# A fifth set of single-row transfers, an own buffer for tile 0, and the diagonals made on VectorE

## The reference

```python
x = x + elu(softmax(leaky(e_src + e_dst) masked by adj) @ (layernorm(x) @ W))
h = layernorm(x)                          # 8 batches of 1024 tokens
scores, idx = product_key_top16(h)        # of 128 + 128 keys: 16 of 16384 rows, per token and head
w = softmax(scores)
k = sum(w[j] * keys_table[idx[j]] for j in range(16))      # per token and head, 128 wide
v = sum(w[j] * values_table[idx[j]] for j in range(16))
x = x + causal_attention(h @ Wq, k, v) @ Wo                # 8 heads, 1024 tokens
```

## Time and profile before

| | |
|---|---|
| time, median of 3 runs | 10059.12 us (10057.98 to 10074.63) |
| profiled execution, its span | 10059.9 us |
| GpSimd busy | 7544.0 us, 75% |
| VectorE busy | 6956.2 us, 69% |
| TensorE matmuls busy | 5726.9 us, 57% |
| ScalarE busy, without issuing DMAs | 3087.9 us, 31% |
| DMA engines' mean busy share | 39% in a steady head |

### The profile page before, as it was taken

One profiled execution on the slowest core, in us unless ns is written; L12 is line 12 of the kernel. 1 busy time (PEld: TensorE's weight loads), 2 busy tenths in 40 slices (PEclk: granted clock), 3 DMA queues, 4 the chain that ended last, 5 costly groups with the idle time before them and its releaser, 6 DMA issues.

```text
span 10059.9 us, 190416 instructions
## 1 busy us (share of the span) xinstructions
PE 5726.9 (57%) x23108; PEld 4551.2 (45%) x23108; DVE 6956.2 (69%) x42844; ACT 3087.9 (31%) x9770; POOL 7544.0 (75%) x7957
## 2 busy tenths in 40 slices
PE   5655555555555555555555555555555555555555
PEld 4544444444444444444444444444444444444444
DVE  8876667666666677676776666767667676666664
ACT  4333233233333333333333333333333332322222
POOL 5777777777777777777777777777777777777776
PEclk7877777777777777777777777777777777777777
DMA  3333343333433334333343333333333333333333
GB/s 109 105 109 109 109 114 109 109 109 109 113 109 109 109 109 113 109 109 109 109 113 109 109 109 109 113 109 109 109 111 111 110 109 109 109 111 109 109 109 100
DMA packets 503669, 1100.92 MB, mean 109 GB/s; under 512 B 196992, under 2 KB 246912, under 8 KB 502144
## 3 DMA queue, kind: packets, MB, share of 16 engines
q0 software_dynamic: 381120, 1041.22, 36.4%
q1 hardware_dynamic: 71488, 31.70, 1.3%
q10 hardware_dynamic: 49664, 16.42, 0.8%
HBM read 1084.36 MB, written 4.19 MB: 108 GB/s over the span
## 4 chain that ended last, share of the span: by engine, by line
POOL 73%; issue 24%; DVE 1%; PE 1%; POOLq 0%; DMA 0%; ACT 0%; ACTq 0%; SPq 0%; DVEq 0%
POOL ring L353 73%; DVE hot L1013 0%; DMA wo<-in_Wo 0%; POOLq L369 0%; PE ps_o L724 0%; ACTq L492 0%; POOLq L367 0%; DVE ps_v L935 0%; DMA ring<-in_table,idx 0%; PE ps_p L610 0%; PE ps_p L614 0%; DVE nmax L1064 0%; PE ps_s L748 0%; POOLq L368 0%; DVE cand L987 0%
## 5 line engine op out<-in xcount | busy, mean ns | idle before, releaser
L353 POOL DMA_INDIRECT ring<-in_table,idx x7940 | 7542.5, 950 | 2491.2 <-issue 2420.6
L671 PE MATMUL ps_w<-ring,diag 128*128 128x256 f32 x8192 | 2151.7, 423 | 13.0 <-issue 8.7
L715 PE MATMUL ps_p<-ident,prob 128*128 128x128 f32 x2304 | 564.7, 400 | 2304.0 <-ACT prob L453 2296.3
L671 PEld LDWEIGHTS ps_w<-ring,diag 128*128 128x128 f32 x8192 | 1740.6, 218 | 297.1 <-issue 19.7
L1013 DVE SCALAR_TENSOR_TENSOR hot<-rank,posf,cand 128x54 f32<-128x54 f32 x8192 | 1654.5, 271 | 0.3
L715 PEld LDWEIGHTS ps_p<-ident,prob 128*128 128x128 f32 x2304 | 395.1, 202 | 2501.0 <-ACT prob L453 1600.2
L932 DVE TENSOR_SCALAR ps_v<-ring,wgt 128x256 f32<-128x256 f32 x512 | 248.4, 485 | 1837.0 <-DMA ring<-in_table,idx 1836.8
L935 DVE SCALAR_TENSOR_TENSOR ps_v<-ring,wgt,ps_v 128x256 f32<-128x256 f32 x3072 | 1478.9, 481 | 19.6
L444 ACT ACTIVATE diag<-ident,wgt 128x128 f32<-128x128 f32 x4096 | 1251.8, 391 | 0.0
L453 ACT ACTIVATE prob<-ps_s,nmax 128x128 f32<-128x128 f32 (+7 forms) x512 | 378.1, 738 | 2300.8 <-issue 2259.6
L724 PEld LDWEIGHTS ps_o<-probT,kv 128*128 128x128 f32 x4608 | 986.7, 304 | 144.9 <-ACT probT L461 81.6
(11 more groups left out here) (119 smaller groups left out, 8141.2 us busy)
## 6 DMA issues: line engine op xcount, KB each, us to landing
far<-in_table SPq DMA_DIRECT2D x16352, 1.0 KB
far<-in_table ACTq DMA_DIRECT2D x15904, 1.0 KB
ring<-in_table,idx POOLq DMA_INDIRECT x7940
xin<-in_x SPq DMA_DIRECT2D x8, 512.0 KB
mask<-in_adj SPq DMA_DIRECT2D x1, 4096.0 KB, 15.9
out_x<-acc SPq DMA_DIRECT2D x64, 64.0 KB
far_row<-far_at SPq DMA_DIRECT2D x128, 0.5 KB
far_row<-far_at ACTq DMA_DIRECT2D x124, 0.5 KB
```

The source lines that it names most:

```text
L353: pool.indirect_dma_start(out=ring[:, t % RING, k, :], out_offset=None, in_=table, in_offset=bass.IndirectOffsetOnAxis(ap=idx[:, t, k:k + ...
L671: ins = nc.tensor.matmul(pw_ps, diag[:, k, :], ring[:, t % RING, k, :], start=(k == 0), stop=(k == PE_ROWS - 1))
L715: ins = nc.tensor.transpose(ps_p[:, c, (j % 4) * P:(j % 4 + 1) * P], prob[:, j * P:(j + 1) * P], ident[:])
```

## The change

- SETS are five tiles: 1, 6, 0, 4 and 3. SyncE fetches tile 1 (128 rows), 96 rows of tile 3, and tile 6 (128 rows); it asks for the next set's addresses ahead of the last 32 rows of the one it fetches. ScalarE fetches tiles 0 and 4 and 32 rows of tile 3, 36 rows in each unit, as 20 and 16 with a register load for each; they are issued in portions of 8 between its other work of the unit (some, with TURNING, TURNED and SUMMING), the rest at the unit's end. ScalarE does this in the first head as well, from unit 4 on.
- The sum of tile 0 is written to kv_first, not to kv[:, 0, :]. ScalarE copies its values to kv later in the unit (keep_first), VectorE's wait for the last product moves to t = 1, and TensorE's last product stands behind turn_keys at t = 0 as at the others.
- VectorE makes all eight diagonals of a unit in one product of 128 x 1024, right behind sum_rows; ScalarE makes none.
- stores and load of SyncE stand at other places of the turn from batch to batch.

```diff
-FAR = (3, 7)
-NEAR = (0, 4)
-SETS = FAR + NEAR
-NEAR_UNITS = 4
+SETS = (1, 6, 0, 4, 3)
+SP_ORDER = (0, 4, 1)
+SP_STOP = {0: P, 4: 96, 1: P}
+SP_FIRST_ORDER = (2, 0, 4, 1)
+NEAR_BEGIN = {1: 2, 4: 4, 5: 3}
+NEAR_PARTS = {1: ((2, 0, (20, 16)),), 2: ((2, 36, (20, 16)),), 3: ((2, 72, (20, 16)),),
+              4: ((2, 108, (20,)), (4, 96, (16,))),
+              5: ((3, 0, (20, 16)),), 6: ((3, 36, (20, 16)),), 7: ((3, 72, (20, 16)),),
+              0: ((3, 108, (20,)), (4, 112, (16,)))}
+ACT_BEGINS = tuple(NEAR_BEGIN.values())
+FIRST_SETS = (3, 4)
+FIRST_UNITS = (4, 5, 6, 7)
+TURNING = 8
+TURNED = 8
+SUMMING = 8
...
+        def made(t):
+
+            return kv[:, t, :] if t else kv_first[:]
...
-            def far_fetch(n, i, stop=P):
+            def far_fetch(n, i, following=None):
...
+                stop = SP_STOP.get(i, P)
                 for q in range(0, stop, LOADED):
+                    if q == stop - LOADED and following and following[1] not in ACT_BEGINS:
+                        far_begin(*following)
...
+            def turn(b, more):
+                n = (b + 1) * HEADS
+                far_fetch(n, SP_ORDER[0], (n, SP_ORDER[1]))
+                if more:
+                    load(b + 2)
+                far_fetch(n, SP_ORDER[1], (n, SP_ORDER[2]))
+                far_fetch(n, SP_ORDER[2], (n + 1, SP_ORDER[0]))
                 stores(b)
...
-            def diagonals(n, t):
-
-                act.wait_ge(pw_mm, n * UNITS + t)
-                act.wait_ge(wgt_ready, n * UNITS + t + 1)
-                for k in range(PE_ROWS):
-                    nc.scalar.mul(diag[:, k, :], ident[:], wgt[:, t, k:k + 1]).then_inc(diag_ready, 1)
...
+            def keep_first():
+
+                nc.scalar.copy(kv[:, 0, P:KV], kv_first[:, P:KV]).then_inc(first_kept, 1)
...
+                    for rows in loads:
+                        _, at = nc.values_load_multi_w_load_instructions(
+                            far_row[0:1, i, start:start + rows], engines=[mybir.EngineType.Activation],
...
+                    some(fetch, TURNING)
                     if t or not first:
                         attend_turned(*behind)
+                    some(fetch, TURNED)
                     if ahead:
                         choose_softmax((n + 1) * UNITS + t)
                     attend_begin(n, t)
...
+                    some(fetch, SUMMING)
                     if t or not first:
                         attend_out(*behind)
+                    if t == 0:
+                        keep_first()
...
+                    some(fetch, P)
...
-                pe.wait_ge(diag_ready, (u + 1) * PE_ROWS)
+                pe.wait_ge(diag_ready, u + 1)
...
+                if t == 1:
+                    pe.wait_ge(first_kept, n + 1)
...
-                if t == 0:
+                if t == 1:
 
                     dve.wait_ge(o_mm, n * UNITS)
                 after(row_sum[0])
-                nc.vector.tensor_tensor(kv[:, t, :], part[:], pw_ps, ALU.add).then_inc(rows_summed, 1)
+                nc.vector.tensor_tensor(made(t), part[:], pw_ps, ALU.add).then_inc(rows_summed, 1)
...
+            def diagonals(n, t):
+
+                dve.wait_ge(pw_mm, n * UNITS + t)
+                dve.wait_ge(wgt_ready, n * UNITS + t + 1)
+                nc.vector.tensor_tensor(diag[:], ident[:].unsqueeze(1).broadcast_to([P, PE_ROWS, P]),
+                                        wgt[:, t, 0:PE_ROWS].unsqueeze(2).broadcast_to([P, PE_ROWS, P]),
+                                        ALU.mult).then_inc(diag_ready, 1)
...
                         sum_rows(n, t)
+                        diagonals(n if t < UNITS - 1 else n + 1, (t + 1) % UNITS)
                         choose_rows(t, a_unit, c)
```

More of the change, by code:

```diff
@@ L1 @@
+import itertools
 from contextlib import ExitStack
@@ L295, in far_fetch, with far_sets @@
                             .then_inc(far_dma[i], 16)
[L297 to L308, removed]
+            def far_sets(n, order, follows):
+                for i, after_it in zip(order, order[1:] + (follows,)):
+                    if i == order[-1]:
+                        far_fetch(n, i, None if follows is None else (n + 1, follows))
+                    else:
+                        far_fetch(n, i, (n, after_it))
@@ L315, in _ @@
[L315 to L321, removed]
+            far_begin(1, SP_FIRST_ORDER[0])
+            far_sets(1, SP_FIRST_ORDER, SP_ORDER[0])
             with sp.Fori(2, HEADS) as h:
-                far_sets(h, range(len(FAR)))
+                far_sets(h, SP_ORDER, SP_ORDER[0])
             with sp.Fori(0, BATCH - 2) as b:
-                load(b + 2)
-                turn(b)
+                turn(b, True)
@@ L327, in _ @@
                 with sp.Fori(1, HEADS) as h:
-                    far_sets((b + 1) * HEADS + h, range(len(FAR)))
-            turn(BATCH - 2)
+                    far_sets((b + 1) * HEADS + h, SP_ORDER, SP_ORDER[0])
+            turn(BATCH - 2, False)
             with sp.Fori(1, HEADS - 1) as h:
-                far_sets((BATCH - 1) * HEADS + h, range(len(FAR)))
-            far_sets(BATCH * HEADS - 1, range(len(FAR)), True)
+                far_sets((BATCH - 1) * HEADS + h, SP_ORDER, SP_ORDER[0])
@@ L473, in near_begin, with near_fetch, some @@
                     act.dma_start(far_row[0:1, i, :], far_at[:, i:i + 1]).then_inc(far_row_dma[i], 16)
-            def near_load(n, i, part):
-                if part in (0, NEAR_UNITS - 1):
+            def near_fetch(n, t, first):
+                for i, start, loads in NEAR_PARTS[t]:
+                    if first and (t not in FIRST_UNITS or i not in FIRST_SETS):
+                        continue
                     act.wait_ge(far_row_dma[i], n * 16)
                     act.sem_inc(act_mark, 1)
[L480 to L493, removed]
+                    if not (isinstance(n, int) and n == 1):
+                        act.wait_ge(rows_summed, (n - 1) * UNITS + SETS[i] + 1)
+                        act.sem_inc(act_mark, 1)
+                    for rows in loads:
+                        _, at = nc.values_load_multi_w_load_instructions(
+                            far_row[0:1, i, start:start + rows], engines=[mybir.EngineType.Activation],
+                            min_val=0, max_val=(HEADS * NUM_KV - 1) * KV_BYTES,
+                            skip_runtime_bounds_check_because="made of two positions below 128 and a head below 8")
+                        for j in range(rows):
+                            yield act.dma_start(far[start + j:start + j + 1, i, :].bitcast(U8),
+                                                table_bytes[bass.ds(at[j], KV_BYTES)]).then_inc(far_dma[i], 16)
+                        start += rows
+            def some(fetch, rows):
+                for _ in itertools.islice(fetch, rows):
+                    pass
             act.wait_ge(aux_mm, 1)
@@ L537, in head @@
                         graph_keep(b + 1, h, g)
-                    if ahead and t in (1, 1 + NEAR_UNITS) and not first:
-                        near_begin(n + 1, len(FAR) + t // NEAR_UNITS)
+                    if ahead and t in NEAR_BEGIN and not (first and NEAR_BEGIN[t] not in FIRST_SETS):
+                        near_begin(n + 1, NEAR_BEGIN[t])
+                    fetch = iter(())
+                    if ahead or t == 0:
+                        fetch = near_fetch(n + 1 if t else n, t, first)
                     if ahead:
@@ L548, in head @@
                     attend_begin(n, t)
[L549 to L555, removed]
-                        near = len(FAR) + (t - 1) % UNITS // NEAR_UNITS
-                        part = (t - 1) % NEAR_UNITS
-                        at = near_load(n + 1 if t else n, near, part)
-                        near_rows(near, part, at, range(0, HIDDEN))
+                    some(fetch, SUMMING)
                     if t or not first:
                         attend_out(*behind)
+                    if t == 0:
+                        keep_first()
                     if ahead:
@@ L567, in head @@
                         graph_copy(g)
-                    if fetch:
-                        near_rows(near, part, at, range(HIDDEN, LOADED))
+                    some(fetch, P)
                 if not ahead:
@@ L682, in turn_keys @@
                     pe.wait_ge(g_xnT_copied, graph_rows[0])
-                nc.tensor.transpose(ps_t[:, 0, :], kv[:, t, 0:P], ident[:]).then_inc(k_tp, 1)
+                nc.tensor.transpose(ps_t[:, 0, :], made(t)[:, 0:P], ident[:]).then_inc(k_tp, 1)
             def scores(n, t):
@@ L722, in attend_sum @@
                 pe.wait_ge(p_copied, halves(n, t) + HALVES[t])
+                if t == 1:
+                    pe.wait_ge(first_kept, n + 1)
                 for j in range(t + 1):
-                    ins = nc.tensor.matmul(oT_ps, kv[:, j, P:KV], probT[:, j * P:(j + 1) * P],
+                    values = kv[:, j, P:KV] if t else kv_first[:, P:KV]
```

(9 more changed lines are left out.)

10 lines of the change are left out of this document (3 added, 7 removed).

## The result

The changed kernel takes 10250.1 us (median of 4 runs, 10237.49 to 10256.0) against 10058.57 us for the kernel before in the same comparison: 1.0187 times as long, 95% interval 1.0172 to 1.0201. It is slower by 1.9%, with the whole interval above 1, as forecast; the forecast was 10209 us, the range 10085 to 10295. The profiled execution spans 10247.8 us, 187.9 us more than that of before.

What follows compares the result with a forecast made beforehand. The prediction took GpSimd's gathers, count times price, to bound the kernel: 10059.9 - 79.1 (fewer gathers) + 216 (gathers stretched by VectorE's products) + 12.5 (start) = 10209 us, range 10085 to 10295.

Steps and rivals of the forecast that it cites:

- The bound: Whole kernel: from 280 us on, time is GpSimd's count of gathers times 1.255 us each, pause included.
- The fifth set: GpSimd's gathers: one fewer in each of 63 heads from the second on, 79.1 us off.
- second rival: VectorE's product: its form doesn't stretch gathers, so the change is what it counts, 9993 us; chance 0.04.
- the seven products of the start: VectorE's products queued ahead of the sum GpSimd waits for at the start: 7 x 1.22 = 8.5 us later.
- The product's wait: Gathers starting under VectorE's diagonal product wait for its stream's end: 502 x 0.43 = 216 us added.
- Other gathers: Gathers not held by the diagonal products: the forecast had no added time for them.
- The start: GpSimd's early wait for VectorE's sum: +12.5 us, 8.5 from seven products and 4 from ScalarE's rows.
- ScalarE's rows in the first head: Units 4 to 7: issuing rows may delay exponentials and VectorE's weights by 0 to 20 us; 4 taken.
- A lucky phase: First rival: VectorE's products fall between two gather starts, so the kernel is faster, 10008 us at 15 us stretch; chance 0.06.
- The form isn't exempt: Answers the second rival, that VectorE's product form stretches no gathers: 9993 us, chance 0.04.
- ScalarE isn't the bound: Answers the third rival: ScalarE's 124 to 155 us of head work sets the time, about 10530 us; chance 0.06.
- The fourth rival: VectorE's product blocks gathers for its whole 1.22 us instruction: 0.59 us a product, 298 us, 10291 us; chance 0.06.

Runs made afterwards that it cites:

- e7: The kernel before with only tile 0's own buffer kv_first, ScalarE's copy, and the moved VectorE wait and TensorE product: 10084.14 us, 0.9999 of the kernel before.
- e2: The changed kernel with the eight diagonals back on ScalarE; five sets, spread rows and own buffer stay: 9993.57 us, 0.9933 of the kernel before.
- e3: The kernel before with only VectorE's single product in place of ScalarE's diagonals, four sets kept: 10292.0 us, 1.0206 of the kernel before.
- e8: The changed kernel with diagonals as eight VectorE products by a scalar copied to PSUM, ahead of the sum: 10025.17 us, 0.9944 of the kernel before.
- e1: The changed kernel with weights copied to PSUM and the product reading them there, ahead of the sum: 10004.37 us, 0.9945 of the kernel before.
- e4: The changed kernel with the 128x1024 product made as two of 128x512, inputs still in SBUF: 10107.98 us, 1.005 of the kernel before.
- e5: The changed kernel with diagonals as eight VectorE products of ident by a scalar read from SBUF: 10027.38 us, 0.9967 of the kernel before.

## Why the prediction was right, point by point

**The bound.** Right: GpSimd alone, before and after. Every time in the table above follows from its count of gathers and what stretches them. The own buffer was costed at nothing, and e7 gives 0.9999.

**The fifth set.** Right: 63 gathers fewer are worth 79 us. With the product's wait left out the prediction's second rival gave 9993 us, and e2, which is that case by another way, took 9993.57. That they agree to the microsecond is chance: the 9993 counts 8.5 us for the seven products of the start, which e2 doesn't have.

**The product's wait: the mis-sized term.** The mechanism held in each of its parts: the wait is at the gather's start, lasts to the stream's end less 0.12 to 0.13 us, and has its ceiling near 1.05 us (1994 - 946), 1.02 ns a column (the 0.275 us that the prediction read over 256 columns is 1.07, not 1.05). The size was 0.455 us a product for all 512, not 0.43 for 502. The prediction had two estimates: starts that fall anywhere, 0.455, and the starts recorded before, 0.41; it went halfway between. The recorded phase was that of a kernel with four sets, and with four sets e3 indeed shows a lower wait, 0.372. The other parts of the change shift the gathers against the sums: unit by unit the mean wait runs from 0.21 to 0.56 us in e3 and only from 0.34 to 0.52 in the changed kernel. Of these parts it is the new sets and their spread rather than the own buffer: a product laid behind the recorded sums, as the prediction did it, would hold gathers for about 0.40 us in e7, no more than before, and for 0.45 in e2 (an estimate from the starts in these two traces). So the two parts of the change weren't independent: beside the product the other parts bring 1.0187 against 1.0206, some 19 us, where without it (e2) they bring 67. Of the difference 42 us are the phase, 512 x (0.455 - 0.372).

**Other gathers: a term that wasn't there.** 20.6 us. Of it choose_rows (L1029, 54 columns a pass) held gathers for 8.0 us more (14.7 to 22.7) and graph_edges for 4.2 more; in e3 choose_rows rose by 5.9 over e7 with the gathers' count unchanged, so some of it comes with the product; that the product pushes these passes to another phase would explain it, but isn't shown. The remaining 8 us are the ordinary gather's own level, 1 to 2 ns higher, which differs between executions and chips (median 949 ns in e3, e7 and e8, 946 in e1 and e4, 947 in e2); between e7 and e3 it doesn't move, and nothing shows that the change made it.

**The start.** 11.9 us for 12.5, by two parts that the runs separate: without products (e2) the wait for the sum is 21.4 us, 8.8 above before, where 4 were taken for ScalarE's rows in the first head. About 6 us of it are a later sum, the rest a GpSimd that gets there sooner. The rows are the likely cause, not a proven one: the own buffer alone (e7) leaves the wait at 12.2 us, and in e2's chain from 180 to 290 us ScalarE's issuing of rows has 20%. The seven products ahead add only 3.1 us to the wait, not 8.5: the sum that is waited for ends 285 us into the span, 278 in e2, but the gathers of the start are stretched too and GpSimd comes 3.3 us later itself. That 8.8 and 3.1 sum to nearly the 4 and 8.5 of the forecast is luck.

**The rivals.** A lucky phase would have had to hold 0.133 us a product. The form isn't exempt, though e1 shows what would have exempted it. ScalarE isn't the bound: beside the five sets it carries the diagonals in e2, and GpSimd waits for a sum only in the start. The fourth rival, a block for the whole instruction, asked for 0.59 us a product; the mean was 0.455, and the gather at 3460.45 was held for 0.57 us, not for the 0.70 that were left of the instruction. The Trainium skill (SBUF — State Buffer, section "SBUF: two separate sides") has whichever of the two starts first hold the pair for its whole instruction while the other is blocked. The trace agrees that each can block the other, but not on how long: the product holds a gather until 0.12 to 0.13 us before its own end, and a gather, 946 ns long, keeps a product waiting for 0.065 us at most (25 of 512 products, up to 1283 ns against 1218), though gathers are under way three quarters of the time.

## What to carry to other kernels

Where one engine's instruction count sets the time, look for what stretches a single one of them before relieving an engine that has time to spare: moving 1252 us of work off a ScalarE that had the time cost 233 us inside GpSimd's gathers. A hold that lasts to the end of a stream costs by the square of the stream's length (two halves cost half: 102 us against 233). Reading the product's second tensor from PSUM took the hold away at the price of a copy of 170 ns; a scalar in PSUM left a small rest (2 us of 21). A phase read from a trace belongs to that kernel's own pitch of instructions. Where the same change alters the pitch, starts that fall anywhere are the safer estimate; here they gave the measured 0.455, which is one case.

## What the runs showed of the hardware that was not expected

A scalar operand of VectorE matters to GpSimd's gathers: passes of 128 columns with the weight in SBUF held them by up to 0.138 us (e5), with the weight in PSUM by up to 0.066 us and only from 0.09 us into the pass on (e8); 358 gathers over 1000 ns against 115.

The hold works both ways. A product of two SBUF tensors that starts within some 0.03 us of a gather's start is itself held until it ends 1.254 to 1.258 us after that start, up to 65 ns late (25 of 512 products; in e3 19, at 1.255 to 1.258). With one tensor in PSUM (e1) neither holds the other.

The ordinary gather isn't equally long everywhere. Its median was 946 ns in e1 and e4 and 949 in e3, e7 and e8; over 7940 gathers 3 ns are 24 us, about what the kernel before differs by between these chips (10060.91 and 10084.06 us). It isn't the chip alone: beside e8, on a third chip, one of the kernel's seven executions took 10061.72 us and the others 10079.85 to 10085.55.
